# A graph-attention kernel: x's remainders and own-node terms moved to VectorE, loads and the operand stage reordered

## The reference

```python
# layer 0
h = einsum('bnf,of->bno', x, W_w) + W_b;  h[:, 0, :] = 0
mask = adj[1:, :] > 0
neigh = einsum('ji,bjf->bif', mask, h[:, :N-1, :])
s = einsum('bif,fi->bi', h, a[:64]) + einsum('bif,fi->bi', neigh, a[64:]);  s[:, 0] = 0
h_prime = s[:, :, None] * h.sum(axis=1)[:, None, :]
x = layernorm(x + where(h_prime >= 0, h_prime, 0.01 * h_prime))
# layer 1: four heads, then one
h = einsum('bnc,hdc->bhnd', x, Wh)
z = leaky_relu(softmax(where(mask1, h @ h.T, -1e16)) @ h + bh, 0.2)      # per batch and head
h2 = einsum('bnk,dk->bnd', z, Wo)
out2 = leaky_relu(softmax(where(mask1, h2 @ h2.T, -1e16)) @ h2 + bo, 0.2)
x = layernorm(x + layernorm(out2) * gamma + beta)
```

## Time and profile before

| | us |
|---|---|
| median of 3 runs | 3126.8 (3121.39 to 3129.04) |
| the profiled execution | 3127.07 |
| its span | 3125.3 |

### The profile page before, as it was taken

How to read it: one execution, slowest core, us unless ns; L and a number is a source line. 1 busy time by engine, 2 the same in 40 slices (tenths; PEclk the granted TensorE clock), 3 DMA queues, 4 the chain that set the end, 5 groups by cost and what they waited for, 6 DMA issues and landing times. The chain is left out here.

```text
span 3125.3 us, 124905 instructions
## 1 busy us (share of the span) xinstructions
PE 2923.1 (94%) x49770; PEld 2168.0 (69%) x49770; DVE 2681.5 (86%) x5523; ACT 2275.4 (73%) x2654; POOL 2587.7 (83%) x1458
## 2 busy tenths in 40 slices
PE   7957999999999999999999999999998889999990
PEld 5435777777777777777777777777776867777760
DVE  6966888888888888988889888988897579999988
ACT  1267777777777777777777777777776567777773
POOL 4465999998898999999999989999999079888882
PEclk8979999999999999999999999999999999999995
DMA  6139899889999889998899898898987878898773
GB/s 245 48 132 342 146 167 165 157 155 161 159 166 163 157 158 168 165 165 158 157 171 165 166 150 160 164 164 168 160 158 144 294 152 158 163 165 163 155 140 89
DMA packets 1443985, 514.30 MB, mean 165 GB/s; under 512 B 1359503, under 2 KB 1417293, under 8 KB 1441357
## 3 DMA queue, kind: packets, MB, share of 16 engines
q1 hardware_dynamic: 1443532, 507.36, 82.7%
HBM read 105.30 MB, written 66.06 MB: 55 GB/s over the span
## 5 line engine op out<-in xcount | busy, mean ns | idle before, releaser
L583 POOL TENSOR_TENSOR low<-probs 128x1024 f16<-128x1024 f32 x1280 | 2395.7, 1893 | 358.3 <-ACT probs L870 255.0
L870 ACT ACTIVATE probs<-scores,shifted_max 128x2048 f32<-128x2048 f32 x640 | 1282.5, 2004 | 223.6 <-DVE shifted_max L1077 219.9
L736 PE MATMUL ps<-operands 128*128 128x512 f16 x2560 | 973.7, 380 | 7.9 <-DMA v_parts<-h_d 5.8
L737 PE MATMUL ps<-operands 128*128 128x512 f16 x2560 | 972.2, 380 | 0.0
L1072 DVE CUSTOM_DVE_ANT_0 scores<-ps,mask,neg_max 128x1024 f32<-128x1024 f32 x640 | 821.6, 1284 | 126.4 <-issue 73.3
L898 ACT COPY probsT<-ps 128x1024 bf16<-128x1024 bf16 x640 | 647.6, 1012 | 374.7 <-PE ps L745 374.7
L745 PEld LDWEIGHTS ps<-ident,probs 128*128 128x128 bf16 x10240 | 650.1, 98 | 370.0 <-issue 202.3
L1072 DVE CUSTOM_DVE_ANT_0 scores<-ps,mask 128x1024 f32<-128x1024 f32 x640 | 781.3, 1221 | 134.1 <-PE ps L737 124.0
L745 PE MATMUL ps<-ident,probs 128*128 128x128 bf16 x10240 | 780.5, 219 | 9.9 <-DVE probsT L1086 6.9
L756 PE MATMUL ps<-v_parts,probsT 128*128 128x64 f16 x10240 | 685.4, 193 | 5.5 <-issue 5.5
L755 PE MATMUL ps<-v_parts,probsT 128*128 128x64 f16 x10240 | 685.0, 193 | 1.4 <-DVE outs L1136 1.4
(11 more groups left out here) (156 smaller groups left out, 1734.7 us busy)
## 6 DMA issues: line engine op xcount, KB each, us to landing
operands<-hT_d SPq DMA_DIRECT2D x40, 512.0 KB, 4.3
operands<-hT_d SPq DMA_DIRECT2D x80, 256.0 KB, 4.0
v_parts<-h_d SPq DMA_DIRECT2D x40, 512.0 KB, 4.9
probsT<-low SPq DMA_TRANSPOSE x1280, 3.5
z_d<-outs SPq DMA_DIRECT2D x38, 512.0 KB, 3.9
h_d<-probs SPq DMA_DIRECT2D x32, 512.0 KB, 5.9
hT_d<-probsT SPq DMA_DIRECT2D x32, 512.0 KB, 5.3
scores<-z_d SPq DMA_DIRECT2D x32, 512.0 KB, 4.9
```

What stands on the lines that cost most here:

```text
L583: pool.tensor_tensor(low[:, u, w], probs[:, u, w], high[:, u, w], ALU.subtract).then_inc(sem(f"low{half}"), 1)
L736: pe.matmul(ps[:, b, :], hi_lo[:, p, t * P:(t + 1) * P], hi_lo[:, p, w], start=True, stop=False)
L737: scored = pe.matmul(ps[:, b, :], hi_lo[:, p, t * P:(t + 1) * P], lo_hi[:, p, w], start=False, stop=True)
L870: act.activation(probs[:, 1 - u, :], scores[:, 1 - u, :], ACT.Exp, bias=shifted_max[:, 1 - u:2 - u], scale=-1.0, accum_out=row_sum[:, held ...
```

## The change

- Loads: W, its two copies and b0 come first on a semaphore of their own (`w0_loaded`), then `a` (`a_loaded`), x in four quarters of 1 MB, one DMA each, over all batches (quarter q is tiles 4q to 4q + 3), in turn with slabs 0 to 2 of adj; Wh and Wo behind slab 0 (`weights_loaded`); bh and the four rows behind slab 1 (`rows_loaded`).
- PE: two f32 products with the constant stand in place of the 123 transposes; W is transposed and `a` multiplied as soon as each is loaded, and Wh and Wo are transposed behind that.
- ACT: the first quarter's high parts come before the copies of `a`'s products.
- DVE makes the remainders (`low_x`, from x times the 0/1 factor `node_on` minus the high part, where POOL subtracted and then cleared row 0), two tiles ahead of each mask, and the own-node products with their reduction behind each mask. POOL has neither any more.
- Unit k of the operand stage is batch k % 8 and tile group k // 8. POOL splits a unit when its four tiles are scaled, the first two inside its loop of powers. PE begins the stage when all sixteen neighbour tiles have been read out of PSUM (`neigh_free`), not when all are scaled. ACT scales tiles 14 and 15 behind the first unit. SP's stores are written out, not looped.

```diff
+        def unit(k):
+
+            return k % B, k // B
@@ SP
+            sp.dma_start(a_in, a).then_inc(sem("a_loaded"), 16)
+
+            def load_x(q):
+                w = slice(q * G * D, (q + 1) * G * D)
+                sp.dma_start(xs[:, :].rearrange("p (b n) -> p b n", b=B)[:, :, w],
+                             x.rearrange("b (p t) c -> p b (t c)", t=NT)[:, :, w]).then_inc(sem(f"x_loaded{q}"), 16)
...
+            load_x(0)
+            load_adj(0)
             sp.dma_start(w_nat[:, D:3 * D].rearrange("p (k c) -> p k c", k=2),
                          wh.rearrange("(k h) d c -> (h d) k c", k=2)).then_inc(sem("weights_loaded"), 16)
             sp.dma_start(w_nat[0:D, 3 * D:7 * D], wo).then_inc(sem("weights_loaded"), 16)
+            load_x(1)
+            load_adj(1)
...
+            load_x(2)
+            load_adj(2)
+            load_x(3)
...
-            with sp.Fori(0, B - 1) as b:
-                serve_units(b)
+            for k in range(UNITS - 4):
+                store_h(k)
+                store_hT(k)
@@ POOL
-            for k in range(NT):
-                pool.wait_ge(sem(f"x_loaded{k // 8}"), 16 * B)
-                pool.wait_ge(sem("hi_made"), k + 1)
-                remainder = pool.tensor_tensor(pair(col(h_lo, k, BD)), x_btc[:, :, k, :], pair(col(h_hi, k, BD)), ALU.subtract)
...
-            pool.wait_ge(sem("a_copied"), 4)
-            for k in range(NT):
-                since(pool, sem("s1_made"), k - 1)
-                pool.tensor_tensor(pair(work[:, k % 2, :]), x_btc[:, :, k, :], aT[:, k:k + 1, 0:D].to_broadcast([P, B, D]),
-                                   ALU.mult).then_inc(sem("s1_prod"), 1)
...
             for i in range(NT):
+                if i == NT - 2:
+                    part_step(0, 0)
+                    part_step(1, 1)
                 w = slice(i % 2 * B, (i % 2 + 1) * B)
                 pool.wait_ge(sem("a_var"), i + 1)
...
-            pool.wait_ge(sem("x1_done"), NT)
...
             for t in range(NT):
-                part_step(2 * t, 0)
-                part_step(2 * t + 1, 1)
+                if t:
+                    part_step(2 * t, 0)
+                    part_step(2 * t + 1, 1)
                 mask_step(t)
@@ PE
-            for _ in range(123):
-                pe.transpose(banks16(7, 1)[:, 0:P], ident_h[:, :], ident_h[:, :])
-            pe.wait_ge(sem("weights_loaded"), 16 * 13)
-
+            for _ in range(2):
+                pe.matmul(ps[:, 7, :].rearrange("p (o n) -> p o n", o=4), ident[:, :], ident[:, :].rearrange("p (o n) -> p o n", o=1).to_broadcast([P, 4, P]),
+                          start=True, stop=True)
+            pe.wait_ge(sem("w0_loaded"), 16 * 5)
...
-            pe.wait_ge(sem("x1_done"), NT)
+            pe.wait_ge(sem("neigh_free"), NT)
             turn_x1(0, 0)
@@ ACT
-            normalize(NT - 2)
-            normalize(NT - 1)
...
+            def first_units(k, w, b):
+                p1_step(k, w, b)
+                if isinstance(k, int) and k == 0:
+                    normalize(NT - 2)
+                    normalize(NT - 1)
@@ DVE
+            def low_x(k):
+                dve.wait_ge(sem(f"x_loaded{k // 4}"), 16)
+                dve.wait_ge(sem("hi_made"), k + 1)
+                dve.scalar_tensor_tensor(pair(col(h_lo, k, BD)), x_btc[:, :, k, :], node_on[:, k:k + 1], pair(col(h_hi, k, BD)),
+                                         ALU.mult, ALU.subtract).then_inc(sem("lo_made"), 1)
...
+            dve.wait_ge(sem("pool_const"), 7)
+            low_x(0)
+            make_mask(0)
             dve.wait_ge(sem("weights_turned"), 1)
...
+            dve.wait_ge(sem("a_copied"), 4)
             for k in range(NT):
...
+                if k:
+                    for j in (2 * k - 1, 2 * k):
+                        if j < NT:
+                            low_x(j)
+                    make_mask(k)
+                v = work[:, k % 2, :]
+                dve.tensor_tensor(pair(v), x_btc[:, :, k, :], aT[:, k:k + 1, 0:D].to_broadcast([P, B, D]), ALU.mult).then_inc(sem("s1_prod"), 1)
+                dve.wait_ge(sem("s1_prod"), k + 1)
+                dve.tensor_reduce(s1[:, k, :], pair(v), AX.X, ALU.add).then_inc(sem("s1_made"), 1)
```

More of the change, by code:

```diff
@@ L320, in _ @@
         def _(sp):
[L321 to L327, removed]
+            sp.dma_start(w_nat[0:D, 0:D], w0).then_inc(sem("w0_loaded"), 16)
             sp.wait_ge(sem("twice_cleared"), 1)
             for k in range(2):
[L330 to L338, removed]
+                sp.dma_start(w0_twice[k * D:(k + 1) * D, k * D:(k + 1) * D], w0).then_inc(sem("w0_loaded"), 16)
+                sp.dma_start(w0_twice[k * D:(k + 1) * D, P + k:P + k + 1], b0.rearrange("(c o) -> c o", o=1)).then_inc(sem("w0_loaded"), 16)
+            sp.dma_start(a_in, a).then_inc(sem("a_loaded"), 16)
[3 more added lines that the diff above has]
+                             x.rearrange("b (p t) c -> p b (t c)", t=NT)[:, :, w]).then_inc(sem(f"x_loaded{q}"), 16)
             def load_adj(k):
@@ L344, in _ @@
             load_x(0)
-            for k in range(3):
-                load_adj(k)
+            load_adj(0)
+            sp.dma_start(w_nat[:, D:3 * D].rearrange("p (k c) -> p k c", k=2),
+                         wh.rearrange("(k h) d c -> (h d) k c", k=2)).then_inc(sem("weights_loaded"), 16)
+            sp.dma_start(w_nat[0:D, 3 * D:7 * D], wo).then_inc(sem("weights_loaded"), 16)
             load_x(1)
+            load_adj(1)
+            sp.dma_start(bh_rows[:, :, :].rearrange("p h d -> p (h d)"),
+                         bh.rearrange("h d -> (h d)").rearrange("(o n) -> o n", o=1).to_broadcast([P, H * D])).then_inc(sem("rows_loaded"), 16)
+            for k, row in enumerate((b0, bo, gamma, beta)):
+                sp.dma_start(rows[:, k, :], row.rearrange("(o c) -> o c", o=1).to_broadcast([P, D])).then_inc(sem("rows_loaded"), 16)
+            load_x(2)
+            load_adj(2)
+            load_x(3)
             for k in range(3, NT):
@@ L395, in _ @@
                 load_part(0, 0, k)
-            serve_units(B - 1)
+            for k in range(UNITS - 4, UNITS):
+                store_h(k)
+                store_hT(k)
             for k in range(OPERAND_DMAS):
@@ L613, in _ @@
             last.then_inc(sem("weights_turned"), 1)
-            for t in range(NT):
-                a_t = a_in.rearrange("f (p t) -> f t p", t=NT)[:, t, :]
-                pe.matmul(ps[:, 2 + t // 4, t % 4 * P:(t % 4 + 1) * P], a_t, w0_twice[:, 0:P], start=True, stop=True)
-                turned = pe.matmul(ps[:, 6, 2 * t:2 * t + 2], a_t, w0_twice[:, P:P + 2], start=True, stop=True)
-            turned.then_inc(sem("a_turned"), 1)
             pe.wait_ge(sem("weights_copied"), 2)
@@ L812, in _ @@
             act.copy(c12[:, :, :], ps[:, 6, 0:2 * NT].rearrange("p (t k) -> p t k", k=2)).then_inc(sem("c_copied"), 1)
-            high_x(0)
-            high_x(1)
+            for q in range(1, 4):
+                high_x(q)
             def normalize(i):
```

79 lines of the change are left out of this document (38 added, 41 removed).

## The result

| | median us | lowest to highest | runs | ratio to before, 95% interval |
|---|---|---|---|---|
| before | 3127.9 | 3121.4 to 3131.7 | 4 | |
| after | 3188.3 | 3174.2 to 3193.4 | 4 | 1.0186 [1.0160, 1.0211] |

The change costs 60 us where 19 us of gain were forecast. The stretches of the profiled execution say where. The columns are those of the earlier trace rows. The first three are the whole neighbour loop (it lasted 62.8 us before, from 39.5 to 102.3; the earlier trace rows shows it from 60.20 on), the pair loop and 74.2 us of the operand stage, these two at the same points of the work as in the earlier trace rows; the row behind the dots is the layer-1 attention loop between its first and its last branch back.

What follows compares the result with a forecast made beforehand. Four serial stretches before the attention loops (88% of the span, length carried over) were taken to bound the gain: 13.2 us to the neighbour loop's end plus 5.5 at the hand-over, 18.7 off, 3108.1 us; range 3099 to 3117.

Steps and rivals of the forecast that it cites:

- Rival (4): Operand stage: stores to blocks further apart slow the DMA engines from 370 to 290 GB/s, 26 us more, 3134; chance 0.04.
- The opening: Start-up until the loops: `a` issued at 3.95, multiplied from 9.45 at half clock; neighbour loop starts at 29.0, against 39.5.
- Rival (1): Start-up: the two f32 products lift TensorE to full clock, 14.05 us become 7.0; 3104, or 3101 if slabs keep up; chance 0.20.
- The neighbour loop: VectorE bounds the first eight turns at 4.32 us, PE the rest; ends at 89.1 against 102.3, a gain of 13.2 us.
- Rival (2): Neighbour loop: VectorE pays towards 1.12 us for each new instruction; gain only 5.1 + 5.5 us, 3116.2; chance 0.11.
- T0: Time at which the neighbour loop can start, worked as 29.0 us, against 39.5 before.
- The pair loop: Between neighbour loop and operand stage: bound by VectorE, unchanged at 83.2 us, only moved earlier.
- The hand-over: Pair loop to operand stage: stage begins 10 us earlier, of which 5.5 us remain; bounds 4.0 and 8.
- Rival (3): Pair loop to operand stage: the earlier beginning gives nothing, units wait for scalings and GpSimd or DMA queue; 3113.6; chance 0.10.
- GpSimd beside VectorE: End of pair loop: splits of units 0 and 1 could cost VectorE up to 2.5 us, 3110.6, by the Trainium skill.

Runs made afterwards that it cites:

- the last experiment: GpSimd splits units 2 and 3 before copying the bias and making mask step 0, against the changed kernel with 24 start-up transposes; 3108.0 us, beside 3111.0.

## Why the prediction was wrong

**The step that failed** is the first sentence of the working: the attention loops are 88% of the span, "the change touches nothing in them and I carry their length over". It took equal code for equal time. The change removes 240 instructions of PE ahead of the loop, and that moved the loop's branch from 207 to 223 of its block: 77 us. No rival held this. Rival (4), the only one on the slower side, named another mechanism (stores) and didn't occur: the operand stage moves 371 GB/s where it moved 370.

**The opening** came out as worked. The rows that answer to the earlier trace rows:

```profile
3.91 0.58 SPq L330 DMA_DIRECT2D v_parts<-in_L_gnn_a  x1
```

```profile
9.28 0.81 PE L605 MATMUL ps<-scratch,v_parts 128*128 128x128 f32 x2 [2.02 <-DMA v_parts<-in_L_gnn_a]
...
23.75 0.63 PE L613 MATMUL ps<-ident,scratch 64*64 64x64 f32 x4
28.58 0.59 PE L623 MATMUL ps<-probs,mask 128*128 128x512 f16 x1 [4.20 <-DVE w L975]
...
31.95 0.62 PE L623 MATMUL ps<-probs,mask 128*128 128x512 f16 x1
32.38 0.41 PE L624 MATMUL ps<-operands,mask 128*128 128x512 f16 x1
```

`a` was issued at 3.91 (worked: 3.95), its products began at 9.28 (9.45) and ended at 23.2 (23.5); the loop began at 28.58 (29.0). Rival (1) is out: the products of `a` took the 0.78 to 0.81 us of the earlier trace rows, which is the lower clock there (0.50), and the rise came only between 31.95 and 32.4, in the neighbour loop. The profile's granted clock reads 1.00 over 9.28 to 23.30, but its first record of the clock in this run begins at 32.43, so ahead of that the durations count and not this share. The rule of the Trainium skill that was set beside this rival (TensorE: Matmul & The Clock Gate, "Part 4: PE-mode transpose") would have favoured it; two f32 products did not lift the clock either.

**The neighbour loop**: VectorE's turn, the rows that answer to the earlier trace rows:

```profile
29.84 1.40 DVE L952 SCALAR_TENSOR_TENSOR operands<-xs,node_on,probs 128x512 f16<-128x512 f32 x2
31.17 1.88 DVE L957 TENSOR_SCALAR mask<-scores 128x2048 bf16<-128x2048 int32 x1
32.97 0.68 DVE L985 TENSOR_TENSOR probsT<-xs,probsT 128x512 f32<-128x512 f32 x1
33.69 0.69 DVE L987 TENSOR_REDUCE s<-probsT 128x8 f32<-128x512 f32 x1
...
35.61 1.92 DVE L957 TENSOR_SCALAR mask<-outs 128x2048 bf16<-128x2048 int32 x1
```

A turn is 35.61 - 31.17 = 4.44 us, worked 4.32: two remainders fill 1.33 us, 0.66 each, where 0.60 was taken between bounds of 0.60 and 1.12. Rival (2) is out. Its price had been worked too low: with 1.12 for remainders and products alike a turn is 5.76 us, mask 8 is done at T0 + 45.0 and the loop at T0 + 71.1, not 68.2, which leaves a gain of 2.2 us and 3119 us; 68.2 is near the sum with 1.12 for the remainders alone. VectorE copies x's sums at 89.80 (worked 89.1), so this part gave 12.5 us and not 13.2. No mask conversion waited for its slab: over this loop the only wait of VectorE in the profile is its last one, for PE's sums.

**The pair loop** took 83.1 us (83.2). **The hand-over**: unit 0 was split by 173.66, in the times of before 186.2 (worked 186); the third high part is at 189.42, which against VectorE's copy of x's sums is 5.4 us nearer than before (5.5). Rival (3) is out. The working of the unit's path held in each step: PE's stop before unit 2's transposes, named there as GpSimd's bias copy and mask step, stands in the trace as `[4.24 <-POOL scores L538]`, and the last experiment takes it away.

Together: 12.5 + 5.4 = 17.9 us worked from the trace of after, where 18.7 was forecast; 17.2 us between the medians with the loop at its old place. So every term of the sum stood within 0.7 us, and the number was 80 us off because of what the sum didn't contain.

**GpSimd beside VectorE.** The splits of units 0 and 1 next to the end of the pair loop:

```profile
171.66 0.68 DVE L1055 SCALAR_TENSOR_TENSOR outs<-small,probsT 128x512 f32<-128x512 f32 x1
172.00 0.60 POOL L535 CAST scores<-xs 128x256 f16<-128x256 f32 x1
172.25 0.88 DVE L1055 SCALAR_TENSOR_TENSOR outs<-small,low 128x512 f32<-128x512 f32 x1
172.77 0.89 POOL L538 TENSOR_TENSOR scores<-xs,scores 128x256 f16<-128x256 f32 x1 [0.18 <-POOL scores L535]
173.61 0.39 POOL L535 CAST scores<-xs 128x256 f16<-128x256 f32 x1
```

The instruction of VectorE with two inputs that runs beside them takes 0.88 us and not 0.68, the splits 0.60 and 0.89 and not 0.39 and 0.67. So both engines give way, by 0.2 us each, once. The Trainium skill (SBUF — State Buffer, "Who interferes with whom") has them shut each other out; by that, up to 2.5 us had been set beside the sum. The direction agrees, and the amount here is 0.2 us, since only one instruction of VectorE still lay beside the splits.

## What to carry to other kernels

A loop that a change doesn't touch may still run differently, because its place in the engine's program has moved. Before a change that adds or removes instructions ahead of a long loop of TensorE, count where its branch back falls in its 256-instruction block, before and after; here the places from 105 to 207 were free, from 215 to 223 a turn cost 3.5 us and more at the lower clock after it, and the gaps were smaller but still there up to 68 of the next block. When a loop slows with the same instructions in it, look for idle time released by "issue" behind the branches and for a changed count of instruction fetches per turn, and try a few instructions more or fewer in a place where they cost nothing before looking for another cause.

## What the runs showed of the hardware that was not expected

- 16 instructions that do nothing, ahead of a loop, cost 67 us of 3127 (ratio 1.0214).
- The branch hint is worth some 74 us in this kernel (3184.6 in one run against 3111.0, on different chips; 76.6 us over the loop in the traces). With it the return is free at place 207 and not at 215, and where the return is free the way out of the loop costs 3.1 to 3.8 us once.
- A stop of 3.5 us costs about 6 us: the products behind it run at the lower clock for a while (0.61 us instead of 0.38), which is 34 of 84 us over the loop.
- 240 semaphore increments on TensorE filled 33 us, so one is some 0.14 us (an estimate). Eight of them in the loop's body made its gap about 1 us longer, which agrees. 16, 64 or 101 of them in PE's wait for GpSimd's first split cost nothing by themselves.
- Two f32 products of 512 columns and 32 f32 products of `a` behind them left TensorE at its lower clock up to 32.4 us, with PE busy from 9.28 to 23.2 without a pause (0.78 us a product at the end as at the start); it rose in the 16-bit products of the neighbour loop.
